# The dense projection of an attention layer in two fp16 parts, its first half placed between the last attention groups

## The reference

```python
x = x + 0.5 * ffn(layernorm(x))        # 512 -> 1792 -> 512, gate and up, silu
x = x + attention(layernorm(x))        # 32 query heads, 8 key/value heads, 16 channels each
x = x + 0.5 * ffn(layernorm(x))
# attention, after softmax(q k^T / 16, causal) v:
ctx = einsum('bhqk,bkhd->bqhd', probs, v).reshape(B, S, 512)
out = einsum('bsh,oh->bso', ctx, w_dense) + b_dense      # the dense projection
```

## Time and profile before

| what | value |
|---|---|
| time, median of 3 runs | 1591.55 us (1591.51 to 1592.71) |
| profiled execution: its own time, its span | 1593.44 us, 1591.7 us |
| granted TensorE clock, mean | 0.967 of full |
| busy share of PE, DVE, ACT, POOL | 92%, 56%, 40%, 10% |
| attention loop, one full iteration | 25.6 us |
| PE's iterations 16 and 17 with the last context | 1039.3 to 1073.7 us |
| dense stage | 1073.7 to 1143.8 us |
| second feed-forward layer | from 1143.8 us |

### The profile page before, as it was taken

One profiled execution on the slowest core, in us unless ns is written; L12 is line 12 of the kernel. 1 busy time (PEld: TensorE's weight loads), 2 busy tenths in 40 slices (PEclk: granted clock), 3 DMA queues, 4 the chain that ended last, 5 costly groups with the idle time before them and its releaser, 6 DMA issues.

```text
span 1591.7 us, 24945 instructions
## 1 busy us (share of the span) xinstructions
PE 1468.1 (92%) x9552; PEld 660.3 (41%) x9552; DVE 886.1 (56%) x1387; ACT 629.0 (40%) x887; POOL 151.2 (10%) x217
## 2 busy tenths in 40 slices
PE   0778999899999895799999999989999999999998
PEld 0233444344445453334343434324444444444443
DVE  7979432432444587899999999923431422412212
ACT  4464111121222133388888888771211212112111
POOL 0320000000000243012121212210000000000000
PEclk9989999899999987599999999999999999999999
DMA  9501800000000000000000000024000000000000
GB/s 388 195 0 53 353 0 0 1 0 0 1 1 0 1 1 34 1 3 2 2 2 3 2 2 2 2 94 185 0 0 0 27 0 0 27 0 0 27 0 27
DMA packets 16459, 57.38 MB, mean 36 GB/s; under 512 B 4848, under 2 KB 4848, under 8 KB 15856
## 3 DMA queue, kind: packets, MB, share of 16 engines
q1 hardware_dynamic: 16368, 56.11, 9.1%
HBM read 40.63 MB, written 15.20 MB: 35 GB/s over the span
## 4 chain that ended last, share of the span: by engine, by line
PE 80%; DVE 12%; ACT 4%; issue 3%; DMA 1%; POOL 0%; DVEq 0%; SPq 0%; ACTq 0%; POOLq 0%
PE ps L1222 32%; PE ps L1243 16%; PE ps L1478 9%; PE ps L1393 7%; PE ps L1459 5%; PE ps L1576 3%; PE ps L1269 2%; PE ps L1216 1%; DVE w_all L870 1%; DVE rowmax L1110 1%; PE ps L1488 1%; PE ps L1355 1%; DVE w_raw L829 1%; DVE wbase L864 1%; ACT parts_q L665 1%
## 5 line engine op out<-in xcount | busy, mean ns | idle before, releaser
L1222 PE MATMUL ps<-xt_hi,w_all 128*128 128x512 f16 x896 | 284.3, 390 | 41.4 <-DVE w_all L870 19.3
L693 ACT ACTIVATE probs<-ps 128x1024 f32<-128x1024 f32 (+3 forms) x384 | 294.2, 814 | 48.7 <-PE ps L1459 45.7
L1110 DVE TENSOR_REDUCE rowmax<-ps 128x2 f32<-128x1024 f32 (+3 forms) x208 | 237.0, 1140 | 16.0 <-PE ps L1401 7.5
L958 DVE SCALAR_TENSOR_TENSOR hb<-ps,scal,silub 128x512 f32<-128x512 f32 x56 | 42.0, 750 | 266.6 <-PE ps L1222 266.6
L1393 PE MATMUL ps<-ka,qa 48*128 48x512 f16 (+3 forms) x768 | 165.6, 345 | 15.4 <-DVE rowmax L1110 9.2
L1222 PE MATMUL ps<-xt_lo,w_all 128*128 128x512 f16 x448 | 174.6, 390 | 0.0
L1478 PE MATMUL ps<-probs,vs 128*32 128x512 f32 (+3 forms) x1536 | 164.5, 500 | 1.6 <-ACT ctx_sb L712 1.1
L1222 PEld LDWEIGHTS ps<-xt_hi,w_all 128*128 128x128 f16 (+1 forms) x896 | 89.7, 100 | 155.5 <-issue 41.3
L1114 DVE TENSOR_REDUCE rowmax<-ps 128x1 f32<-128x512 f32 x192 | 131.1, 683 | 16.3 <-PE ps L1393 13.5
L1459 PE MATMUL ps<-qa,ka 50*128 50x512 f16 (+3 forms) x768 | 133.2, 330 | 3.7 <-ACT probs L693 2.8
L1243 PE MATMUL ps<-w32b_all,hhib 128*128 (+1 forms) x448 | 133.3, 379 | 0.0
(11 more groups left out here) (148 smaller groups left out, 2151.7 us busy)
## 6 DMA issues: line engine op xcount, KB each, us to landing
spill<-w_all SPq DMA_DIRECT2D x1, 10752.0 KB, 28.8
w32b_all<-spill SPq DMA_DIRECT2D x1, 7168.0 KB, 19.6
x<-x_in SPq DMA_DIRECT2D x4, 1024.0 KB, 5.4
y_out<-x SPq DMA_DIRECT2D x4, 1024.0 KB, 4.2
wbase<-m1t SPq DMA_DIRECT2D x4, 896.0 KB, 12.6
w_raw<-w1t SPq DMA_DIRECT2D x4, 896.0 KB, 14.1
wbase<-m3t SPq DMA_DIRECT2D x4, 896.0 KB, 24.3
w_raw<-w3t SPq DMA_DIRECT2D x4, 896.0 KB, 24.3
```

The source lines that it names most:

```text
L693: nc.scalar.activation(probs[u % PBUF][:, 2 * pair:2 * pair + 2, 0:q1 - q0], wide(("scores", g, (u, pair)))[:, :, 0:q1 - q0], ACT.Exp, sca ...
L958: nc.vector.scalar_tensor_tensor(out=bufs["h"][u][:, :], in0=ps[:, UP, :], scalar=scal[:, 1:2], in1=bufs["silu"][u][:, :], op0=ALU.mult, o ...
L1110: nc.vector.tensor_reduce(dst, src, AX.X, ALU.max).then_inc(pair_taken, 1)
L1222: last = mm(ps[:, bank, :], w[a][:, k, bass.ts(t, P)], xt[b][:, k, :], start=(k == 0 and n == 0), stop=(k == HB - 1 and n == 2))
```

## The change

- **The arithmetic.** The dense weight is scaled by a power of two and split into a high and a low f16 part; the context too. `project` does three f16 products in place of one f32 product. The ones column of `vs`, by which the context is normalised, carries a power of two as well, and the result is scaled back when it is added to x (`add_dense`).
- **Preparing the weight, inside the attention loop.** DVE reduces the weight to its largest magnitude at the end of iteration 0 (`dense_bound`), POOL reduces that over the partitions, and DVE works out the scale at the end of iteration 1 (`dense_scale`). POOL scales and copies the high parts in iteration 2 (`dense_high`, four times two instructions) and subtracts for the low parts in iteration 3 (`dense_low`, four instructions), both after `copy_v`. SP moves the parts to their place with four DMAs after the row maxima of group 4.
- **The order.** The loop on PE and DVE ends at iteration 15. What iterations 16 and 17 held is written out on PE with the 8 tiles of the first sequence between it: `transpose_rows(0..8)` through bank 4 and `project(0..7)`, quarter by quarter, into bank 5. One bank each, so both wait for the tile before. DVE does the copies of the context (`context_high`, `context_low`), the bias and `add_dense`.
- **The second sequence** follows in a loop as before, with `context_high` on ACT, `context_low` on DVE, and two banks each. `layer_norm(8)` stays behind tile 8's addition.

```diff
+        def dense_high(n):
...
+            if n == 0:
+                pool.wait_ge(wd_scaled, 1)
+            chain(nc.gpsimd.tensor_scalar(wd_raw[:, n, :], wd_raw[:, n, :], wc[:, 3, 3:4], None, ALU.mult))
+            nc.gpsimd.tensor_copy(wd_at[n // 2][:, n % 2, :], wd_raw[:, n, :]).then_inc(wdhi_ready, 1)
...
+        def dense_low(n):
...
+            pool.wait_ge(wdhi_ready, n + 1)
+            nc.gpsimd.tensor_tensor(out=wd_at[2 + n // 2][:, n % 2, :], in0=wd_raw[:, n, :], in1=wd_at[n // 2][:, n % 2, :],
+                                    op=ALU.subtract).then_inc(wdlo_ready, 1)
...
         for k in range(GROUPS + 2):
...
             copy_v(k)
+            if k == 2:
+                for n in range(HB):
+                    dense_high(n)
+            if k == 3:
+                for n in range(HB):
+                    dense_low(n)
             mask_unit(k - 1, 2)
...
+        def dense_bound():
...
+            dve.wait_ge(wd_loaded, 32)
+            nc.vector.tensor_reduce(part[:, 3, 1:2], wd_raw[:, :, :].rearrange("p t n -> p (t n)"), AX.X, ALU.max,
+                                    apply_absolute_value=True)\
+                .then_inc(part_ready, 1)
...
+        def dense_scale():
...
+            dve.wait_ge(allr_ready, 9)
+            chain(nc.vector.tensor_copy(wc[:, 3, 1:2], allr[:, 3, 1:2]))
+            power_of_two(3)
+            chain(nc.vector.tensor_tensor(out=scal[:, 4:5], in0=wc[:, 3, 4:5], in1=wc[:, 4, 4:5], op=ALU.mult))
+            nc.vector.tensor_copy(wc[:, 3, 1:2], allr[:, 3, 1:2]).then_inc(wd_scaled, 1)
...
+        def context_low(i):
+            dve.wait_ge(ctx_hi_ready, i + 1)
+            hi, lo = (t[:, :, :].rearrange("p a b -> p (a b)") for t in ctx_t[i % 2])
+            nc.vector.tensor_tensor(out=lo, in0=ps[:, rows_bank(i), :], in1=hi, op=ALU.subtract).then_inc(ctx_lo_ready, 1)
...
+        add_dense(7)
+        context_low(SEQ_TILES)
+        for i in range(SEQ_TILES, TOKEN_TILES):
+            if i + 1 < TOKEN_TILES:
+                context_low(i + 1)
+            add_dense(i)
             if i == 8:
                 layer_norm(8)
...
         def transpose_rows(i):
...
+            if i == 0:
+                pe.wait_ge(pair_taken, NPAIR * GROUPS)
+            elif i <= SEQ_TILES:
+                pe.wait_ge(ctx_lo_ready, i)
...
+        def project(i, q):
+            if i == 0 and q == 0:
+                pe.wait_ge(wd_placed, 64)
+            if q == 0:
+                pe.wait_ge(ctx_hi_ready, i + 1)
+                pe.wait_ge(ctx_lo_ready, i + 1)
+                if 0 < i < SEQ_TILES:
+                    pe.wait_ge(x2_ready, i)
...
+            for n, (a, b) in enumerate(PASSES):
+                last = mm(ps[:, dense_bank(i), :], ctx_t[i % 2][a][:, q, :], wd[b][:, q, :], start=(q == 0 and n == 0),
+                          stop=(q == HB - 1 and n == 2))
...
+        scores_t(14, 7, 0)
         transpose_rows(0)
+        project(0, 0)
+        values(14, 5)
+        scores_t(14, 7, 1)
+        project(0, 1)
+        scores_t(14, 8, 0)
+        transpose_rows(1)
+        scores_t(14, 8, 1)
+        project(0, 2)
+        values(14, 6)
+        transpose_rowmax(15)
+        scores_t(14, 9, 0)
+        project(0, 3)
+        scores_t(14, 9, 1)
+        project(1, 0)
...
```

More of the change, by code:

```diff
@@ L745, in _, with context_high @@
             exps(k - 1, 6, 1)
-        def take_ctx_t(i):
+        def context_high(i):
             act.wait_ge(dt_full, i + 1)
[L750 to L756, removed]
+            act.wait_ge(dense_full, i - 1)
+            nc.scalar.copy(ctx_t[i % 2][0][:, :, :].rearrange("p a b -> p (a b)"), ps[:, rows_bank(i), :])\
+                .then_inc(ctx_hi_ready, 1)
+        for i in range(SEQ_TILES, TOKEN_TILES):
+            context_high(i)
             if i in (12, 13):
@@ new lines, in _ @@
+        context_high(0)
+        context_low(0)
+        bias_x(0)
+        bias_x(1)
+        context_high(1)
+        context_low(1)
+        bias_x(2)
+        bias_x(3)
+        add_dense(0)
+        context_high(2)
+        context_low(2)
+        bias_x(4)
+        bias_x(5)
+        add_dense(1)
+        context_high(3)
+        context_low(3)
+        bias_x(6)
+        bias_x(7)
+        normalise(14, 0)
+        add_dense(2)
+        context_high(4)
+        context_low(4)
+        bias_x(8)
@@ new lines, in _ @@
+        bias_x(9)
+        add_dense(3)
+        normalise(14, 1)
+        context_high(5)
+        context_low(5)
+        bias_x(10)
+        bias_x(11)
+        add_dense(4)
+        normalise(15, 0)
+        context_high(6)
+        context_low(6)
+        bias_x(12)
+        bias_x(13)
+        add_dense(5)
+        context_high(7)
+        context_low(7)
+        bias_x(14)
+        bias_x(15)
+        add_dense(6)
+        normalise(15, 1)
+        add_dense(7)
+        context_low(SEQ_TILES)
@@ L1493, in _ @@
             transpose_qk(0, o)
-        for k in range(GROUPS + 2):
+        for k in range(GROUPS):
             scores_t(k - 2, 7, 0)
@@ L1567, in transpose_rows @@
             for q in range(HB):
-                last = tr(ps[:, 4 + i % 2, q * P:(q + 1) * P], context[:, tt, q, b, :], ident[:, :])
+                last = tr(ps[:, rows_bank(i), q * P:(q + 1) * P], context[:, tt, q, b, :], ident[:, :])
             last.then_inc(dt_full, 1)
[L1571 to L1577, removed]
@@ new lines, in _ @@
+        scores_t(14, 7, 0)
+        transpose_rows(0)
+        project(0, 0)
[12 more added lines that the diff above has]
+        project(1, 0)
+        values(14, 7)
+        scores_t(14, 10, 0)
+        project(1, 1)
+        values(14, 8)
@@ new lines, in _ @@
+        scores_t(14, 10, 1)
+        transpose_rows(2)
+        values(14, 9)
+        scores_t(14, 11, 0)
+        project(1, 2)
+        scores_t(14, 11, 1)
+        project(1, 3)
+        values(14, 10)
+        scores_t(15, 0, 0)
+        project(2, 0)
+        scores_t(15, 0, 1)
+        project(2, 1)
+        values(14, 11)
+        scores_t(15, 1, 0)
+        transpose_rows(3)
+        transpose_context(14, 0)
+        scores_t(15, 1, 1)
+        project(2, 2)
+        values(15, 0)
+        scores_t(15, 2, 0)
@@ new lines, in _ @@
+        project(2, 3)
+        scores_t(15, 2, 1)
+        project(3, 0)
+        scores_t(15, 3, 0)
+        project(3, 1)
+        values(15, 1)
+        scores_t(15, 3, 1)
+        transpose_rows(4)
+        scores_t(15, 4, 0)
+        project(3, 2)
+        values(15, 2)
+        scores_t(15, 4, 1)
+        project(3, 3)
+        scores_t(15, 5, 0)
+        project(4, 0)
+        values(15, 3)
+        transpose_context(14, 1)
+        scores_t(15, 5, 1)
+        project(4, 1)
+        scores_t(15, 6, 0)
@@ new lines, in _ @@
+        transpose_rows(5)
+        values(15, 4)
+        scores_t(15, 6, 1)
+        project(4, 2)
+        scores_t(15, 7, 0)
+        project(4, 3)
+        transpose_context(15, 0)
+        values(15, 5)
+        scores_t(15, 7, 1)
+        project(5, 0)
+        scores_t(15, 8, 0)
+        project(5, 1)
+        scores_t(15, 8, 1)
+        transpose_rows(6)
+        values(15, 6)
+        scores_t(15, 9, 0)
+        project(5, 2)
+        scores_t(15, 9, 1)
+        project(5, 3)
+        values(15, 7)
@@ new lines, in _ @@
+        scores_t(15, 10, 0)
+        project(6, 0)
+        values(15, 8)
+        scores_t(15, 10, 1)
+        project(6, 1)
+        values(15, 9)
+        scores_t(15, 11, 0)
+        transpose_rows(7)
+        scores_t(15, 11, 1)
+        project(6, 2)
+        values(15, 10)
+        values(15, 11)
+        transpose_rows(8)
+        project(6, 3)
+        project(7, 0)
+        transpose_context(15, 1)
+        project(7, 1)
+        project(7, 2)
+        project(7, 3)
+        for i in range(SEQ_TILES, TOKEN_TILES):
```

77 lines of the change are left out of this document (54 added, 23 removed).

## The result

The changed kernel takes 1617.7 us, median of 4 runs (1616.06 to 1621.52), beside 1591.97 (1591.51 to 1592.71): 1.0164 times as long, 95% interval 1.0151 to 1.0177. Slower was forecast; 25.7 us slower was not. The profiled execution takes 1616.5 us with a span of 1614.7, 23.0 more than the 1591.7 before.

What follows compares the result with a forecast made beforehand. PE was taken to bound the kernel (80% of the chain). The terms -10.4 behind the loop, +9.4 preparation and +5.1 clock gave +4.1 us, less 0.7 caught up: median 1595 us, range 1586 to 1601.

Steps and rivals of the forecast that it cites:

- `dense_bound`, iteration 1: DVE's reduction of the weight ahead of group 1's first reduction: costs 2.0 us (0 to 2.3).
- `dense_scale`: Nine short DVE operations ahead of group 2's first reduction: cost 1.6 us (0 to 1.8).
- `dense_high`, the operations: Eight POOL instructions after `copy_v`, 5.3 us together, delay unit 2's mask: PE waits 3.0 us.
- `dense_low`: Four POOL subtractions, 5.0 us together, ahead of a mask: PE waits 2.8 us, or 4.5 at the medians.
- clock, three drops forecast, five seen: Half clock after the 5.9 us wait and two of three waits near 3 us: 5.1 us (1.7 to 8.5).
- behind the loop, without clock: From 1039.3 to the second feed-forward layer: work 77.9 plus waits 16.2 is 94.1 us, 10.4 less than 104.5.
- caught up; start of the loop: Part of the attention loop's 9.4 us comes back as ACT and DVE catch up while PE waits: 0.7 us off.
- the cases on the faster side: Two rivals: preparation and halves cancel, 1591 us (chance 0.32); preparation hidden, 1586 us (chance 0.24).
- the case of the hidden preparation: Rival in the attention loop: 5.8 us of POOL waits vanish with their clock drops, 1586 us; chance 0.24.
- Contended POOL and every drop: Rival: slower `dense_low` and `dense_high` on POOL, and every wait costs the clock, 1600 us; chance 0.14.
- The f16 products do save: Judges the rival that they don't: a dense tile still takes 3.4 us, 13 us added, 1608 us; chance 0.02.

Runs made afterwards that it cites:

- e1: The changed kernel with one tiny POOL scaling added directly behind the reduction over partitions; 1609.19 us.
- e2: The kernel before, with four tiny POOL instructions behind `copy_v`: a scaling in iterations 5, 9 and 11, a reduction over partitions in 7; 1607.8 us.
- e8: The changed kernel with one tiny POOL scaling behind the last mask of the group before, in iteration 2; 1609.61 us in one run.
- e4: e3 with tile 8's layer normalisation cut into four steps, one behind each of the additions 8 to 11; 1585.76 us.
- e3: e1 with `dense_high` (half in iteration 2, half in 3) and `dense_low` (iteration 4) moved to POOL's long gap behind the masks; 1593.6 us.
- e6: e4 with `dense_scale` spread over nine reductions of iteration 1, and PE's first transposes and first product behind the loop put later; 1579.69 us.

## Why the prediction was wrong

The direction and the places of PE's waits were right, the size was not: +3.4 us of span forecast, +23.0 measured. The direction was a weak call, since 3.4 us is hardly more than the 3.2 that can be told from no change. By the terms of the sum:

| term | predicted | measured | shown by |
|---|---|---|---|
| `dense_bound`, iteration 1 | 2.0 | 2.4 | table; the reduction took 2.27 |
| `dense_scale` | 1.6 | 1.6 | PE's wait 1.57 |
| `dense_high`, the operations | 3.0 | 6.6 | e1: PE's wait 6.64 |
| code load in front of it | 0 | 7.2 | e1, e2, e8 |
| `dense_low` | 2.8 | 2.2 | PE's wait 2.22 |
| clock, three drops forecast, five seen | 5.1 | up to 12.5 | 5.2 + 3.0 in iterations 2 and 3, 4.3 behind the loop (99.1 - 90.2 - 4.6) |
| behind the loop, without clock | -10.4 | -7.9 | e4, with the 4.6 us of waits that it removes |
| caught up; start of the loop | -0.7 | -1.7 | this execution's start |

- **The step that failed is `dense_high`: 3.0 us forecast, 13.85 measured.** The sum lets it start at the end of `copy_v` with nothing in front of it, and prices each instruction as a mask: "No row has exactly these; the nearest one-input row of this size is the mask, 0.63 us." The copies to f16 took 0.61, as priced; the scaling took 1.56. The upper bound of 1.2 us for an instruction, 7.5 for the wait, did hold the operations (a mean of 1.1, 6.6 us).
- **What no bound held is the 7.22 us in front of it.** It was to be read before: ahead of the first subtraction of the preparation, POOL stands idle for 7.01 us with nothing to wait for, right behind a reduction over partitions. I read POOL's groups and minima, and not what stood in front of the first instance. The timeline of POOL in the kernel before:

```profile
78.51 0.44 POOL L439 PARTITION_ALL_REDUCE allr<-part  x1
85.96 3.37 POOL L433 TENSOR_TENSOR w_raw<-w_raw,wbase 128x1024 f32<-128x1024 f32 x1 [7.01 <-issue]
```

  The change adds a reduction just before the loop, and I called it tiny and covered. It was (0.38 us); the turn back was not.
- **The subtraction was right.** Four in 4.50 us, 1.13 each for the 1.26 taken, so the choice of the minima over the medians held, though not for the reason given. The trace of the kernel before has a DVE instruction with two SBUF inputs beside nearly all of these minima too (at 45.81 beside L433's 2.35 us, at 542.47 beside L463's 0.85); it began just after POOL's. The number held, and with it the reading of the Trainium skill (SBUF — State Buffer, "Who interferes with whom"): DVE reduced from PSUM there, and nothing was contended. The ends of `dense_low`'s range were 2.8 and 4.5 us.
- **The clock.** I priced a drop at 1.7 us from one pair of rows, and took three; there were five. Behind the loop the price was near: 1.8 for the one at its start (99.1 - 97.3, where e3 has the same waits and no drop) and 2.5 to 3.2 behind the layer normalisation (e3 against e4). Iteration 2's two and iteration 3's one cost up to 8.2 us beyond the waits. A drop seen here lasted from 4 us (686 to 690 in the changed kernel) to 10 us (the same place in e4), and in it PE does half the work. The section of the Trainium skill that I cited (TensorE: Matmul & The Clock Gate, "HAM oscillation") describes a kernel whose waits between bursts are some 3 to 5 us long, and doesn't state that waits as short as most of mine drop the clock. In the changed kernel waits of 1.57 and 2.22 us did, and in e3 and e4 one of 1.64 did not.
- **Behind the loop, 2.5 us less was saved than worked out.** The waits were near: 2.8 us at the start for 2.9, 3.0 for 3.8 on the one bank, 0.84 for 1.1 at the handover, 5.96 for 5.9 behind the layer normalisation; all together 14.6 for 16.2. So was the pitch: three f16 matmuls of a quarter and the two of the score pair behind them start within 1.07 us, 0.214 each. What was off is the work, 77.9 us: in e4, counted from the same point as the forecast's 94.1, PE is busy for 82.0 of 92.0 us, 4.1 more. 1.0 of these are the transposes, 0.56 us from start to start on average (0.44 to 0.64) for my 0.5. The rest probably lies in how I added up, which is argued and not shown: the same sum for the kernel before (26.5 + 16 x 3.87 + 1.8 = 90.2) falls 3.6 short of its busy time of 93.8 us in the earlier trace rows, yet I subtracted my sum from a measured length. I should have made both by one method. Which instructions hold these us, I did not take apart.
- **The rivals.** Neither of the cases on the faster side was what happened, and the case of the hidden preparation was priced too low: with POOL's work out of the way alone (e3) the kernel takes 1593.6 us, not 1586, and is level with the one before. Only with the layer normalisation cut as well, and then the other waits, is it faster, by 0.4 to 0.8% (e4 to e6). "Contended POOL and every drop" had the drops right and the contention wrong. The f16 products do save: 12 of them take 2.6 us from start to start (1108.77 to 1111.36 in e4), where the f32 product took 3.44.

The earlier start of the loop, and 1.2 us of difference between the change's own medians and profiles, are left as scatter between executions. The part of iteration 2's 5.2 us that is clock and the part that is restarting the pipeline I have not separated.

## What to carry to other kernels

Before an engine with loadable code gets a new operation, look in the trace for idle time that ends in "issue" ahead of the first instance behind each change of operation, not at the mean of its group; if there is one, pay it early with an instruction of one element, where the engine is idle. New instructions belong in the longest gap of their engine, cut to its size, and a long block on DVE (8 us of layer normalisation) goes in steps behind the instructions that others wait for. A saving is the difference of two sums made the same way, the old one checked against the measured busy time.

## What the runs showed of the hardware

- POOL needed 5.80 us to turn to a reduction over partitions and 6.84 to 7.22 to turn back to a scaling or subtraction; copies and masks ran with either. The page of the profile shows none of it; the view by source line has two events of 11 ns in POOL's queue where it begins.
- A scaling on POOL by a value per partition, 128x512 f32, took 1.56 us; the cast to f16 of the same size 0.61, the mask 0.63, the subtraction of two such inputs 1.13.
- A wait of 1.57 to 1.59 us was enough for PE to come back at 1.2 GHz, for 4 us in one kernel and for 10 in another at the same place, while the 1.82 us of the earlier trace rows and the 1.64 in e3 and e4 cost nothing.
